# A two-layer GRU with a mixture of experts on one core: the one-bank gate steps at places 7 and 15 in place of 4 and 12, layer 0's projection at 7 and 12

## The reference, cut to what matters

```python
def step(h, xt):                       # one GRU layer, T = 1024 steps
    hg = h @ Whh.T + bhh
    r = sigmoid(xr + hr); z = sigmoid(xz + hz)
    n = tanh(xn + r * hn)
    return (1.0 - z) * n + z * h
h1 = gru(tanh(x @ W_in.T + b_in + ctx)); h2 = gru(h1)
x = x + (gate * h2 + h2) @ W_out.T + b_out
shared = (silu(x @ w1) * (x @ w3)) @ w2
routed = sum over the two best experts e of gates[e] * (gelu(x @ W1e[e]) @ W2e[e])
x = x + (shared + routed) / 3
```

## Time and profile before

| | us |
|---|---|
| median of 3 runs | 2171.57 |
| lowest and highest | 2167.13, 2173.28 |
| the profiled execution | 2161.73 |
| its span | 2159.9 |

### The profile page before, as it was taken

The page is one execution under the profiler, slowest core; times in us unless marked ns, Lnnn a source line. Parts: engine busy times, 40 slices in busy tenths (PEclk is TensorE's granted clock), DMA queues, the critical chain, the costliest instruction groups (busy, mean ns, idle before and its releaser), DMA issues.

```text
span 2159.9 us, 162405 instructions
## 1 busy us (share of the span) xinstructions
PE 2053.9 (95%) x70040; PEld 1501.7 (70%) x70040; DVE 1816.7 (84%) x11343; ACT 1128.4 (52%) x6471; POOL 563.5 (26%) x2542
## 2 busy tenths in 40 slices
PE   6999999999999999999999999999999999999987
PEld 4666667777677776777767776777767776777766
DVE  3888888888888888988888888888888888888874
ACT  2555555555555555555555555555555555555542
POOL 1222232222322223222232222222232222222220
PEclk9999999999999999999999999999999999999998
DMA  5000000000000000000000000000000000000000
GB/s 221 5 5 5 5 5 5 4 5 5 10 5 5 5 5 10 5 5 5 10 5 5 5 5 10 5 5 5 5 10 5 5 5 10 5 5 9 5 5 9
DMA packets 7184, 24.32 MB, mean 11 GB/s; under 512 B 1584, under 2 KB 3904, under 8 KB 6208
## 3 DMA queue, kind: packets, MB, share of 16 engines
q1 hardware_dynamic: 6464, 13.93, 1.7%
HBM read 11.83 MB, written 2.10 MB: 6 GB/s over the span
## 4 chain that ended last, share of the span: by engine, by line
PE 71%; DVE 19%; ACT 7%; issue 3%; DMA 0%; SPq 0%; POOL 0%; POOLq 0%; DVEq 0%
PE bank L336 34%; PE bank L328 20%; PE bank L268 14%; DVE bank L407 6%; DVE cells L427 5%; ACT factors L477 5%; DVE z_pre L408 3%; PE bank L309 3%; DVE r_pre L398 3%; ACT cells L481 2%; DVE bank L416 0%; PE bank L275 0%; DMA x_t<-in_x_t 0%; DVE x L683 0%; DVE n_second L383 0%
## 5 line engine op out<-in xcount | busy, mean ns | idle before, releaser
L336 PE MATMUL bank<-w_h,cells 128*22 128x128 f32 (+4 forms) x32768 | 1377.8, 281 | 21.2 <-DVE cells L427 11.7
L336 PEld LDWEIGHTS bank<-w_h,cells 128*22 128x22 f32 (+4 forms) x32768 | 865.4, 111 | 127.4 <-DVE cells L427 81.2
L328 PEld LDWEIGHTS bank<-w_h,cells 128*2 128x2 f32 (+15 forms) x28112 | 524.2, 113 | 482.5 <-DVE cells L427 454.5
L522 POOL TENSOR_SCALAR cells<-cells 128x4 f32<-128x4 f32 x2048 | 466.7, 228 | 1497.2 <-DVE cells L427 1496.4
L328 PE MATMUL bank<-w_h,cells 128*2 128x64 f32 (+15 forms) x28112 | 779.4, 225 | 67.8 <-DVE cells L427 55.2
L471 ACT ACTIVATE n_second<-r_pre 128x4 f32<-128x4 f32 x2048 | 426.4, 208 | 517.1 <-DVE r_pre L398 474.4
L477 ACT ACTIVATE factors<-z_pre 128x4 f32<-128x4 f32 x2048 | 429.4, 210 | 473.9 <-DVE z_pre L408 427.0
L427 DVE TENSOR_TENSOR_SCAN cells<-factors,cells 128x18 f32<-128x18 f32 x2048 | 396.5, 194 | 215.5 <-ACT cells L481 140.3
L407 DVE STREAM_TRANSPOSE bank<-bank 128x64 f32<-128x64 f32 x2048 | 522.2, 255 | 56.5 <-PE bank L336 35.0
L398 DVE STREAM_TRANSPOSE r_pre<-bank 128x64 f32<-128x64 f32 x2048 | 483.1, 236 | 34.0 <-PE bank L328 23.5
L408 DVE STREAM_TRANSPOSE z_pre<-bank 128x64 f32<-128x64 f32 x2048 | 428.1, 209 | 0.0
(11 more groups left out here) (90 smaller groups left out, 604.3 us busy)
## 6 DMA issues: line engine op xcount, KB each, us to landing
x_t<-in_x_t SPq DMA_DIRECT2D x4, 512.0 KB, 6.6
w_1e<-in_w_1e SPq DMA_DIRECT2D x1, 2048.0 KB
w_2e<-in_w_2e SPq DMA_DIRECT2D x1, 2048.0 KB
w_x<-in_w_x SPq DMA_DIRECT2D x2, 768.0 KB, 8.1
w_h<-in_w_h SPq DMA_DIRECT2D x2, 768.0 KB, 9.9
w<-in_w SPq DMA_DIRECT2D x3, 512.0 KB
out_y<-y SPq DMA_DIRECT2D x6, 256.0 KB, 3.2
w_in<-in_w_in SPq DMA_DIRECT2D x1, 256.0 KB, 2.3
```

The costliest lines, as they stand in the source:

```text
L328: mm = pe.matmul(r_sums[l][p][32 * g:32 * g + B * (j + 1)], state_tile(l, j, kt), w_h[l][:, kt, g, 2 * U:], start=False, stop=False, tile_ ...
L336: mm = pe.matmul(sums[l][p][32 * g:32 * g + B * (j + 1), 0:width], state_tile(l, j, kt), w_h[l][:, kt, g, 0:width], start=False, stop=Fals ...
L522: pool.tensor_scalar(cell_part(step_rows(l, j), 3), cell_part(step_rows(l, j), 1), 0.5, None, ALU.mult)\
```

## The change

The one-bank form moves from places 4 and 12 to 7 and 15, and from slot 896 on from 0, 4, 8 and 12 to 3, 7, 11 and 15. The first piece of layer 0's projection moves from place 4 to 7; the second stays at 12, where the steps now have the two-bank form. The sparse groups put no product at place 12. In the last three groups, part 1 of place 4 becomes free for products and part 1 of place 7 is no longer. Nothing is computed that was not computed before.

```diff
--- before.py
+++ after.py
@@ -43,12 +43,12 @@
 
 
     s = t + LAG * l
-    return s % CH not in ((0, 4, 8, 12) if s >= SHORT else (4, 12))
+    return s % CH not in ((3, 7, 11, 15) if s >= SHORT else (7, 15))
 
 
 def projection_pieces(l):
 
-    return {4: 0, 12: 1} if l == 0 else {0: 0, 1: 1}
+    return {7: 0, 12: 1} if l == 0 else {0: 0, 1: 1}
 
 
 def mixing_pieces():
@@ -87,7 +87,7 @@
 
         j, part = (h // 2 + self.begin) % CH, h % 2
         if engine == "pe":
-            return j in projection_pieces(part ^ 1) or part == 1 and (self.sparse or self.window > 5 * CH and j % 8 != 6)
+            return j in projection_pieces(part ^ 1) or j == 12 and self.sparse or part == 1 and (self.sparse or self.window > 5 * CH and j % 8 != 6)
         if engine == "act":
             return ((j - LAG) if part else j) % CH == 2 or self.sparse and part == 1
         return (j, part) in ((13, 0), (1, 1), (2, 1)) or self.sparse and (j, part) == (14, 0)
```

## The result

Over 19 runs of each kernel, the median is 2173.70 us after and 2169.05 us before. One run of each kernel took some 3.8 ms in a slow state and is left out of the ratio. The ratio is 1.0027, with a 95% interval of 1.0017 to 1.0038: by it the changed kernel is slower by some 5.9 us (3.7 to 8.2); the two medians differ by 4.7. The sign is the predicted one and the time lies in the range. The size lies between the forecast's +8 and nothing, just inside the 0.3% that the prediction called no change, an outcome to which it gave 0.34 against 0.46 for slower.

A forecast was written before the change was run, and what follows sets the result against it. The prediction took the recurrence as the bound and summed -2 (forms), +9.1 (projection), +1 (later groups' products) and 0 (stalls) to +8 us, set on the median: 2179.5 us, +0.37%, range 2162 to 2193.

The forecast's parts named there:

- The bound: Whole kernel: the recurrence of matmuls, then VectorE's and ScalarE's turns, sets the time; products are nearly free (31.58 against 31.35 us).
- The forms: One-bank form moved: places 4 and 12 regain 0.22 us each, 7 pays 0.22, 15 pays 0.19; -2 us over 63 chunks.
- The projection at 12: Projection piece behind a two-bank step: slot 13's layer 0 step starts 0.15 us late; 0.145 us a chunk, +9.1 us.
- the prediction's own case: Sixth group, product behind layer 1's step: layer 0's next step 0.28 us late, slot 15 pays 0.24 of it.
- The product at 12: Sparse groups without product at place 12: 0.43 us leaves TensorE's queue; otherwise the delay would be about 0.24, not 0.18 to 0.19.
- Its +1 for the later groups: 15 chunks of later groups, where a product can still stand at place 12: another 0.07 us each, +1 us.
- The stalls: TensorE waits of 37.9 us in 91 places, read as the instruction queue not keeping up; change taken as 0, bounds -20 and +15.
- Shrinking stalls: Rival, chance 0.17: stalls at places 8 to 14 and 0 to 6 shrink; with half gone, 2160 to 2168 us.
- the hidden delay: Rival, chance 0.13: the delay at slot 13 is hidden, leaving only -2 + 1; about 2170 us, no change.
- the free form at 15: Rival, chance 0.05: 32-column loads pace the two-bank step, so the one-bank form is free at place 15; -2 in all, 2170 us.
- a change that doesn't act: Rival, chance 0.02: the plan can't absorb moved products and delays spill into the tail; a few us either way.
- Growing stalls: Rival, chance 0.13: more slots of 144 instructions make stalls grow by a third; +12 us, 2192 us.

## Why the prediction was right, point by point

**The bound.** Right: the recurrence, with TensorE's order of the two layers' steps, sets a chunk. Products are nearly free in TensorE's time: with half of each product's columns gone the time stays (0.9991). Their instructions aren't free: the mean of a full chunk lies 1.1 us above that of a quiet one. The good chunk of 31.58 us that the prediction took is one without a stall.

**The forms.** Right, and to about a hundredth. Places 4 and 12 gave back 0.22, place 7 took 0.22, place 15 took 0.20 (0.19 predicted). The rival that had the form free at place 15 has fallen, since that slot went from 1.97 to 2.17. It was built on the load time that "TensorE: Matmul & The Clock Gate" of the Trainium skill, section "LDWEIGHTS (loading the stationary operand)", states by columns.

**The projection at 12: the term that was mis-sized.** The step is "I take 0.145 us a chunk". The delay itself was right, 0.13 of 0.15 in quiet chunks and 0.16 in a full one. What it costs at the end is 0.08 quiet and 0.13 full. Two sentences behind it failed. First, the prediction took 0.24 of 0.28 as the rate at which delay turns into time, from a slot where the delay was twice as long. What a late step wins back is no rate: its r group takes 0.22 us instead of 0.27, 0.045 at this place for a delay of 0.13 as for one of 0.17, and the 0.28 - 0.24 = 0.04 of the prediction's own case is the same amount. 0.13 - 0.045 and 0.17 - 0.045 give the 0.08 and 0.13. Second, it expected layer 1's scan to be late by as much, queued behind a late r turn. In the timeline above it comes at 202.10, 1.05 behind layer 0's, as before: with 0.13 rather than 0.28 of delay the r turn was still ahead of it, and layer 1 paid its 0.08 one slot later. With the chunk counts of above, 35 x 0.13 + 20 x 0.08 = 6 us, where the prediction had 9 for all 63 chunks. In the last eight slot 13 is 0.08 longer as well, but the eight together are no longer than before.

**The product at 12.** The direction was right, the size too small: the rule saved some 10 us (1.0075 against 1.0027, each with its interval) and not the 0.06 a chunk that the delays alone would give. The prediction owes its closeness in part to this rule being in the change: without it the cost would have been some 16 us. Its +1 for the later groups isn't seen: the last eight chunks are 1.1 us shorter in the profile. That is no effect of the late move either, since the run with one piece at 7, whose late forms are those of before, has 264.80 us there.

**What was left out.** The tail. Behind the last of the 63 chunks the two profiles have 2171.6 - 2102.4 = 69.2 us and 2159.9 - 2089.0 = 70.9. Of layer 1's last 19 slots four are of the one-bank form instead of five, which at 0.22 us is a small part of it. The run with the forms at 7 and 12 has five of them and 68.2 us, so a gain here isn't shown. Nor is the 1.4 us ahead of the chunks an effect of the change: that stretch varies from 48.8 to 53.4 us over the kernels of this study.

**The stalls.** Taken as 0 with -20 to +15. The waits rose by some 7 us in the profiled pair and moved to places 4 to 7; sums of waits vary by as much without the time following, so that they grew at all is argued, not shown. The reason given, that the instruction stream sets them, is now shown: by the packets of the instruction queue that they follow, by three times the stalls where the one-bank slots are gone and quiet chunks are shorter, and by the same stalls where TensorE's load is cut. "Runtime: NRT & Kernel Launch" of the Trainium skill, section "Instruction fetch mechanics", calls the crossing of a block mostly hidden. The prediction denied that too broadly: in the kernel before only 77 of 548 fetches are followed by such a wait, which is mostly hidden by count, though not free. Without the one-bank slots it is 264 of 585, 109.6 us, and there the traces and the page part.

**The rivals.** Shrinking stalls, the hidden delay, the free form at 15 and a change that doesn't act are excluded by the slot lengths and by the run with one piece at 7. Growing stalls may hold in a small part, by a few of the 12 us.

**The size against the median.** +8 was set on a median, and +5.9 (3.7 to 8.2) was measured. The slot lengths give -1 for the forms and +6 for slot 13, together 5. What is left is 1 us with an uncertainty of over 2, for the stalls, the last chunks and the tail together; no run tells these apart.

## What to carry to other kernels

Work queued between two recurrent steps is free only while the engine is done with it before the next step's input is ready, so put it where the other chain's step is short or where its slot is long anyway, and count that slack from the timeline before moving it. A delay is paid less what the late step catches up, a fixed amount and not a share: here 0.03 to 0.045 us. A delay short of the next queued turn reaches the other chain one step later. Where waits end with nothing shown in the densest instruction streams, a form of fewer instructions can be worth more than its own latency, and where it stands seems to matter as well as how often, which these runs don't settle. Before moving a form, look for a wait in the program that it would pull to the front of the step.

## What the runs showed of the hardware

- Waits before weight loads that nothing in the profile ended follow the fetch of instructions: 64 of 66 (before), 90 of 90 (after) and 219 of 222 (no one-bank form) of those in the steps end 1.2 to 1.7 us after the end of a packet of the instruction queue.
- Without the one-bank slots (64 TensorE instructions more in each) the kernel lost 80 us, with 117.4 us of such waits, in 280 places, 0.42 us each.
- Products of 128 or 64 stationary columns between steps of 32-column groups waited 146 us in 687 places before their weight loads, 0.21 us each. Products in groups of 32 columns, with 4 and 2 times the instructions, waited 10.9 us in 25 places, and the kernel with them was 100 and 78 us faster in all.
- A recurrent step that starts 0.13 or 0.17 us late issues its first 16 matmuls over 0.22 us instead of 0.27.
- The same form of a step costs 0.20 us at place 15 and 0.21 to 0.22 at 4, 7 and 12.
